# Edge stage of a graph layer rebuilt on one Trainium2 core: node-major sums, one-hot stationary, pieces in place

## The reference, cut to what matters

```python
xn = _layernorm(x)
msg = relu(xn[src] + edge_attr)                 # 106250 x 256
h = xn + zeros.at[dst].add(msg)                 # the node sums
h = relu(batchnorm(h @ W1 + b1)) @ W2 + b2      # 256 -> 512 -> 256, then graph norms
q, k, v = split(xn @ W_qkv + b_qkv)             # q, k centred over channels
k2 = k*k / (sum_c(k*k) + 1e-7); k2 = k2 / norm of k2 over the nodes
q2 = q*q / (sum_c(q*q) + 1e-7); q2 = q2 / norm of q2 over the channels
mix = (v + q2 @ (k2.T @ v) / sqrt(6250)) @ W_out + b_out
x = x + (xn + relu(norms(h))) + mix
x = x + mixture_of_8_experts(_layernorm(x))     # top 2 of 8, hidden 682
```

## Time and profile before

| | |
|---|---|
| median of 3 runs | 2623.18 us (2623.16 to 2633.58) |
| span of the profiled execution | 2627.9 us |
| busy: PE, DVE, ACT, POOL | 1897.2, 1206.7, 818.4, 1251.6 us |
| edge stage, first gather issue of its block to the first issue of the next stage | 92.8 to 1445.2 us |
| `up` of the MLP stage on PE | 1455.1 to 1542.3 us |
| granted clock of the whole span | 0.815 |

### The profile page before, as it was taken

The page is one execution under the profiler, slowest core; times in us unless marked ns, Lnnn a source line. Parts: engine busy times, 40 slices in busy tenths (PEclk is TensorE's granted clock), DMA queues, the critical chain, the costliest instruction groups (busy, mean ns, idle before and its releaser), DMA issues. The chain is left out here.

```text
span 2627.9 us, 43936 instructions
## 1 busy us (share of the span) xinstructions
PE 1897.2 (72%) x12178; PEld 1621.3 (62%) x12179; DVE 1206.7 (46%) x3382; ACT 818.4 (31%) x1643; POOL 1251.6 (48%) x1126
## 2 busy tenths in 40 slices
PE   3566677677665677677775889663429999999993
PEld 3455555446555666566665778552318888888883
DVE  5444444445444554454454344563315445445441
ACT  5122222222221222222222345622314444444441
POOL 1566677667666766666664000225752222222221
PEclk7677788778777887777777899556759999999997
DMA  9555555546455665565554800667932232232234
GB/s 207 181 173 170 169 183 185 166 162 205 160 168 173 197 203 178 176 201 174 185 188 138 252 0 0 179 162 195 261 91 41 44 48 45 44 48 45 44 48 114
DMA packets 234810, 368.27 MB, mean 140 GB/s; under 512 B 96291, under 2 KB 184245, under 8 KB 221332
## 3 DMA queue, kind: packets, MB, share of 16 engines
q1 hardware_dynamic: 147689, 205.63, 25.4%
q0 software_dynamic: 74288, 155.59, 22.2%
q10 hardware_dynamic: 12795, 6.60, 1.3%
HBM read 286.51 MB, written 74.69 MB: 137 GB/s over the span
## 5 line engine op out<-in xcount | busy, mean ns | idle before, releaser
L497 POOL DMA_INDIRECT gathered<-xn_rows,src_index x824 | 908.5, 1103 | 433.6 <-issue 262.7
L729 PE MATMUL bank<-dst_select,message 128*128 128x128 f32 x3328 | 530.9, 318 | 278.4 <-issue 149.2
L729 PEld LDWEIGHTS bank<-dst_select,message 128*128 128x128 f32 x3328 | 494.4, 230 | 359.8 <-issue 291.1
L1637 PE MATMUL bank<-rowsT_parts,expert_weights 128*128 128x256 f16 x3564 | 409.5, 274 | 10.1 <-issue 6.2
L1604 POOL DMA_INDIRECT output_rows<-expert_out,token_index x108 | 167.7, 1553 | 475.3 <-DVE token_index L1757 446.5
L1637 PEld LDWEIGHTS bank<-rowsT_parts,expert_weights 128*128 x3564 | 346.1, 98 | 59.8 <-issue 18.0
L620 ACT ACTIVATE message<-message 128x2048 f32<-128x2048 f32 x104 | 198.7, 1910 | 522.6 <-DVE message L576 327.8
L576 DVE TENSOR_TENSOR message<-gathered,edge_attr 128x2048 f32<-128x2048 f32 x104 | 238.4, 2292 | 201.0 <-DMA gathered<-xn_rows,src_index 171.3
L1650 PE MATMUL bank<-expert_weights,gated_parts 128*128 x1836 | 209.3, 273 | 0.6 <-DVE gated_parts L1752 0.6
L1744 DVE SCALAR_TENSOR_TENSOR gated<-bank,silu 128x512 f32<-128x512 f32 x216 | 120.7, 559 | 163.7 <-ACT silu L1682 162.7
L1650 PEld LDWEIGHTS bank<-expert_weights,gated_parts 128*128 128x128 f16 x1836 | 179.5, 98 | 21.7 <-issue 0.9
(11 more groups left out here) (254 smaller groups left out, 2225.1 us busy)
## 6 DMA issues: line engine op xcount, KB each, us to landing
edge_attr<-in_edge_attr SPq DMA_DIRECT2D x104, 1024.0 KB
dispatched_rows<-empty_row SPq DMA_DIRECT2D x2, 7410.0 KB, 35.7
rows<-dispatched_rows SPq DMA_DIRECT2D x55, 260.0 KB
gathered<-xn_rows,src_index POOLq DMA_INDIRECT x832
xnT_tile<-xnT SPq DMA_DIRECT2D x100, 125.0 KB
raw_weights<-in_L_ffn_w SPq DMA_DIRECT2D x16, 640.0 KB
out<-output_rows SPq DMA_DIRECT2D x1, 6250.0 KB, 21.8
rows_to_send<-token_rows ACTq DMA_DIRECT2D x10, 568.8 KB
```

The costliest lines, as they stand in the source:

```text
L497: pool.indirect_dma_start(out=GA[h][:, e, :], out_offset=None, in_=k.xn_d[:, :], in_offset=bass.IndirectOffsetOnAxis(ap=IDX[h][:, e:e + 1] ...
L729: last = pe.matmul(PE_[h][:, c * WIN:(c + 1) * WIN], MSG[h][:, e, c * 128:(c + 1) * 128], SEL[h][:, e, :], start=e == 0, stop=e == EK - 1)
L1637: last = pe.matmul(bank[:, jj * TT:(jj + 1) * TT], w(e, wp, at + b * step, 128), X16[h][:, xp, b, :], start=n == 0, stop=n == 3 * CB - 1)
```

## The change

- The node sums are held node-major: `node_sum` has 128 nodes on the partitions, 50 tiles of 256 channels. The layernorm writes its rows straight there (7 groups of 7 tiles of 128 rows) and stores them from there; ACT makes only the copy to `xnT`, two tiles at a time.
- The tables come as 104 rows of 1024, are cast on DVE and turned on PE. Gathers take their index from `src_table` itself, and batches 0 and 1 are both issued in the layernorm stage.
- In the edge stage the one-hot is the stationary operand and the message the moving one, 256 columns. The one-hot is made on `dst_partition`, the destination's place in its tile modulo 128, and DVE adds the window to two tiles (`into_tiles`), with a mask in each.
- The add is done in place in `edge_attr`, in 8 instructions of 256 elements; there are three buffers of `edge_attr`.
- The key sums are taken over the normalized rows instead of the values (`rows_in`, loaded again from HBM); the value and output weights are applied once, after the sums (`key_weights`). The second pass makes queries and values node-major, turns the squares on PE, and adds the biases by a matmul with one row.
- All loops of both stages are unrolled. The semaphores of both stages are cleared and freed with one more barrier.
- `up` turns `node_sum` first: 4 transposes and a DVE copy for each of 25 chunks of 256 nodes.

```diff
 def layernorm_stage(k, st):
-    G = 10
-    NG = NT // G
+    G = 7
+    NG = PT // G
...
         def _(pool):
...
-            pool.tensor_copy(k.IDX[0][:, :], k.src[:, 0, :]).then_inc(idx_first, 1)
...
+            pool.wait_ge(src_ready, 2)
+            pool.wait_ge(xn_st, 16 * (NG + 1))
+            for b in range(2):
+                gather(k, pool, b, b)
...
+            for n, work in enumerate((None, table_floats, bases, centred, turned_weights, locals_, products)):
+                norm(n)
+                if work:
+                    work()
...
 def edge_mix_stage(k, st):
         @block.gpsimd
         def _(pool):
-                    pool.wait_ge(idx_ready, b)
-                    pool.wait_ge(added, b + 1)
-                    pool.sem_inc(gathers_begun, 1)
+            for b in range(2, NB):
+                pool.wait_ge(added, b - 1)
+                gather(k, pool, b, b % 2)
         @block.vector
         def _(dve):
+            def add(b):
+                ea, ga = EA[b % 3], GA[b % 2]
+                dve.wait_ge(ea_in[b % 3], 16 * (b // 3 + 1))
+                dve.wait_ge(g_in[b % 2], 16 * EK * (b // 2 + 1))
+                for e in range(EK):
+                    last = dve.tensor_tensor(ea[:, e, :], ga[:, e, :], ea[:, e, :], ALU.add)
+                last.then_inc(added, 1)
...
+                for j, here in enumerate((k.here, k.next)):
+                    u = k.UTn[:, bass.ds(at + j, 1), :].rearrange("p a c -> p (a c)")
+                    last = dve.scalar_tensor_tensor(u, WINP[b % 2][:, 0:C], here[:, b:b + 1], u, ALU.mult, ALU.add)
...
-                    dve.tensor_tensor(MSG[h][:, :, :], GA[h][:, :, :], EA[h][:, :, :], ALU.add).then_inc(added, 1)
-                    dve.tensor_copy(IDX[h][:, :], k.src[:, bass.ds(b + 2, 1), :].rearrange("p a k -> p (a k)")).then_inc(idx_ready, 1)
...
+            for b in range(NB):
+                select(b)
+                if is_tile(b - P2 - 2):
+                    residual(b - P2 - 2)
+                add(b)
+                if b > 0:
+                    into_tiles(b - 1)
+                if is_tile(b - P1):
+                    key(b - P1)
+                if is_tile(b - P1 - 1):
+                    scaled(b - P1 - 1)
         @block.tensor
         def _(pe):
+            def scatter(b):
+                pe.wait_ge(sel_done, b + 1)
+                pe.wait_ge(relu_done, b + 1)
+                if b >= 2:
+                    pe.wait_ge(evac, b - 1)
+                for e in range(EK):
+                    last = pe.matmul(WINP[b % 2][:, 0:C], SEL[b % 2][:, e, :], EA[b % 3][:, e, :], start=e == 0, stop=e == EK - 1)
+                last.then_inc(win_full, 1)
...
-                    for c in range(CB):
-                        for e in range(EK):
-                            last = pe.matmul(PE_[h][:, c * WIN:(c + 1) * WIN], MSG[h][:, e, c * 128:(c + 1) * 128], SEL[h][:, e, :],
-                                             start=e == 0, stop=e == EK - 1)
...
 def gnn_mlp_stage(k, st):
+            def turn(c, h):
...
+                        last = pe.transpose(TP[h][:, b * UP + j * NP:b * UP + (j + 1) * NP],
+                                            k.UTn[:, 2 * c + j, b * 128:(b + 1) * 128], k.ident[:, :])
```

More of the change, by code:

```diff
@@ L387, in edge_mix_stage @@
+            for n, work in enumerate((None, table_turns, base_rows, None, weight_products, None, None)):
+                turn(n)
+                if work:
+                    work()
 def edge_mix_stage(k, st):
     nc, sb, sem, A = k.nc, k.sb, k.sem, k.A
-    two = range(2)
-    EA = [sb(f"edge_attr{h}", [128, EK, C], F32, st) for h in two]
-    GA, IDX, g_in = k.GA, k.IDX, k.g_in
-    MSG = [sb(f"message{h}", [128, EK, C], F32, st) for h in two]
-    SEL = [sb(f"dst_select{h}", [128, EK, WIN], F32, st) for h in two]
@@ L444, in on @@
-    def on(eng):
-        def wrap(f):
-            f.eng = eng
-            schedule(f)
-            return f
-        return wrap
-    def held(eng):
-        eng.wait_ge(ready, READY)
+    two, three = range(2), range(3)
+    EA = [sb(f"edge_attr{h}", [128, EK, C], F32, st) for h in three]
+    GA, g_in = k.GA, k.g_in
+    SEL = [sb(f"dst_select{h}", [128, EK, NP], F32, st) for h in two]
+    XT = [sb(f"rows_in{h}", [128, C], F32, st) for h in two]
+    KB = [sb(f"key{h}", [128, C], F32, st) for h in two]
@@ L529, in kv_scale, with select @@
-            def kv_scale(t, h):
-                dve.wait_ge(ks_done, t + 1)
-                dve.wait_ge(kv_used, t + 1)
-                dve.tensor_scalar(RS[h][:, :], KS[h][:, :], EPS_DIV, None, ALU.add)
+            def select(b):
+                h = b % 2
+                if b >= 2:
+                    dve.wait_ge(win_full, b - 1)
+                for e in range(EK):
+                    last = dve.tensor_scalar(SEL[h][:, e, :], k.iota[:, :], k.dstp[:, b, e:e + 1], None, ALU.is_equal)
+                last.then_inc(sel_done, 1)
@@ new lines, in keys, with key_sums @@
+            def keys(t):
+                v, h = rows_of(t), t % 2
+                if t >= 2:
+                    pe.wait_ge(kb_done, t - 1)
+                for c in range(CB):
+                    last = pe.matmul(KP[h][0:v, 0:C], k.XNT[:, t, c, 0:v], k.wk[:, c, :], start=c == 0, stop=c == CB - 1)
+                last.then_inc(kp_full, 1)
+            def key_sums(t):
+                v, h = rows_of(t), t % 2
+                pe.wait_ge(rs_done, t + 1)
+                pe.wait_ge(k4_done, t + 1)
+                first, done = t == 0, t == PT - 1
+                for q in range(CB):
+                    pe.matmul(MP[q][:, 0:C + 1], K2[t % 3][0:v, q * 128:(q + 1) * 128], VS[h][0:v, :],
+                              start=first, stop=done, skip_group_check=True)
+                pe.matmul(NRM[0:1, 0:C], k.ones[0:v, 0:1], K4[h][0:v, :], start=first, stop=done, skip_group_check=True).then_inc(kv_used, 1)
@@ new lines, in _ @@
+            for b in range(NB):
+                if is_tile(b - P1):
+                    keys(b - P1)
+                if is_tile(b - P1 - 2):
+                    key_sums(b - P1 - 2)
+                if is_tile(b - P2):
+                    query_value(b - P2)
+                if is_tile(b - P2 - 1):
+                    query_turns(b - P2 - 1)
+                if b == FIN:
+                    key_weights()
+                scatter(b)
+                if is_tile(b - P2 - 1):
+                    mixed(b - P2 - 1)
@@ L734, in stray_stage @@
+            for t in range(NB - P2 - 1, PT):
+                query_turns(t)
+                mixed(t)
 def stray_stage(k, st):
```

985 lines of the change are left out of this document (544 added, 441 removed).

## The result

The change took 2668.91 us (median of 4 runs, 2656.88 to 2678.08) against 2628.38 for the kernel before: ratio 1.0156, 95% interval 1.0103 to 1.021. So it is slower, by about 1.6%, where the forecast was 2447. The profiled execution has a span of 2667.6 us against 2627.9.

What follows compares the result with a forecast made beforehand. It took POOL's gather issues in the edge stage, plus holds and gaps, to bound the kernel. 2627.9 + 8.5 (head) - 198 (edge stage) + 12 (tail) + 1 (barrier) = 2451.4, less 4.7 for the median: 2447 us, range 2370 to 2565.

Steps and rivals of the forecast that it cites:

- POOL's own price: Edge stage: POOL's 8 gather issues plus the pieces' hold were to take 10.4 us a batch.
- PE's 27 instructions a batch: Edge stage: PE's instruction count was to fall from 48 to 27 a batch.
- my +12: Tail: the 98 transposes ahead of `up`, with the first turn and copy, were to add 12 us.
- rival F: Transposes don't keep PE's clock up and `up` runs at half speed: 2545 us, chance 0.03.
- the gaps: Edge stage: POOL's idle time from PE's slow stretches, 14 of 4.8 us, +67 us.
- rival C: Edge stage: slow stretches limit columns, not instructions, 10.3 us a gap, 14 times: 2524 us, chance 0.18.
- my own case: Edge stage: a slow stretch limits instructions, 33 in 24 us, costing 4.8 us each; 2405 to 2490 us, chance 0.40.
- Rival E: Edge stage: slow stretches come more often because gathers come denser: 2706 us, chance 0.06.
- B: Edge stage: no gap left, as clock or queue recovers with fewer PE instructions: 2380 us, chance 0.17.
- the head: Layernorm stage up to the third batch's first issue: +8.5 us (-10 to +12), first gather at 82 us.

Runs made afterwards that it cites:

- e13: The change itself, unaltered, timed again on another chip: 2457.97 us, 0.9888 of the kernel before.
- e4: The change with 6 of each batch's 8 sums on PE left out, 15 PE instructions a batch instead of 27: 2591.2 us (before in that set: 2606).
- e1: The change with DVE's residual tile moved behind the add and the window adds: 2672.5 us (before in that set: 2606).
- e3: The change with only an eighth of `edge_attr` loaded from batch 3 on: 2664.9 us (before in that set: 2606).
- e2: The change with the add in one instruction of 2048 elements instead of 8 pieces: 2555.7 us (before in that set: 2606).
- e7: The kernel before with only its add split into 8 instructions of 256 elements: 2806.2 us (before in that set: 2671).
- e18: The change with the residual tile behind the add, as in e1, on a chip without slow stretches: 2453.0 us (before in that set: 2483).
- e9: The one-add version e2 with each table loaded as 96 and 7 rows: 2497.8 us (before in that set: 2483).
- e5: The one-add version e2 with 7 more one-column DVE instructions behind the add: 2604.8 us, first half 575.4 us (before: 2671).
- e8: The one-add version e2 with loads of `x` moved ahead of tables and weights, table work later: first half 576.5 us, total not given.
- e6: The change with a 1024-column fill and a drain on POOL ahead of each batch's gathers: 2807.8 us (before in that set: 2671).
- e10: The change with 5 one-column fills on POOL ahead of each batch's gathers, no drain: 2463.1 us (before in that set: 2483).
- e16: The one-add version e2 timed again beside the change, e13, on one chip: 2535.2 us (before in that set: 2485).

## Why the prediction was wrong, step by step

**Right.** POOL's own price: 10.4 us a batch (10.38 here, 10.4 in e13's first half). PE's 27 instructions a batch ((1242 + 1466) / 102 = 26.5 in the windows above). `up`: first turn at 1481.8, last product done at 1579.1, 97.3 us against 87.2, +10.1 for my +12; rival F is out, since its clock with the turns was 0.99. The Trainium skill (SBUF — State Buffer, Who interferes with whom) infers that `tensor_tensor` doesn't stall descriptor generation; issues of 2.24 us beside one add and 2.96 us beside eight pieces contradict it, as in the earlier trace rows.

**The step that failed: the gaps.** "If a stretch limits instructions, the change gets 33 / 27 = 1.22 batches through" and "at one in 78 us": I took the stretches as given from outside, at a fixed rate, and took each to cost what PE falls behind in it: 14 of 4.8 us. The runs show two things in its place. First, nearly halving PE's instructions did not shorten the gaps: the nine of the first half are 10.4 us on average, in before the seven were 9.3, and in the row 209.00:230.00 PE has 19 instructions in 21 us, or 22 in 24, near the 20 that I had set for rival C and not the 33 of my own case. C's price of 10.3 us a gap came out there; its total (2524) did not. e4 goes further: with 15 instructions a batch the gaps remain, and DVE creeps too, so the limit isn't PE's instructions or columns alone. Second, the stretches answer to the pieces, and so to how POOL issues: on one chip e1 and e3 have 19 long gaps each and e2, with one add, has one; in e7 pieces alone go with 453.9 us of idle time. POOL's idle time for the add was 262.9 us instead of 67. With it the edge stage gave 15 us instead of 198, and these 183 us are most of the 216 between the forecast (-176 on the span) and the measurement (+40). Rival E came nearest, "more often, because gathers come denser", with 0.06 and a price too high (2706 us); e7 bears it out, while the change itself had 19 long gaps against 17. On two other chips none of it is there. That is B's outcome, no slow gaps, but not B's reason: the kernel before, with 48 PE instructions a batch, has none there either.

**The second: a ring that I did not look for,** a round of waits that leads from an operation through other engines to its next instance. I read the new order on DVE (one-hot, residual, add) and said only that the engines stay under 10.4 us. But the residual waits for the mix product, that stands on PE behind the scatter, that waits for relu, that for the add. In the change's second half, the profile on the other chip (e13) shows one turn, from one add to the next:

```profile
1153.85 2.76 DVE L623 TENSOR_TENSOR edge_attr<-gathered,edge_attr 128x256 f32<-128x256 f32 x8
1156.65 1.91 ACT L720 ACTIVATE edge_attr<-edge_attr 128x2048 f32<-128x2048 f32 x1 [0.18 <-DVE edge_attr L623]
1158.66 5.38 PE L795 MATMUL bank<-edge_attr,dst_select 128*128 128x256 f32 x16 [2.61 <-issue]
1164.94 0.48 DVE L695 SCALAR_TENSOR_TENSOR residual_tile<-bank,query_scale,rows_in 128x256 f32<-128x256 f32 x1 [5.44 <-PE bank L860]
1165.84 0.42 DVE L623 TENSOR_TENSOR edge_attr<-gathered,edge_attr 128x256 f32<-128x256 f32 x1
```

From 1153.85 the next add comes at 1165.84: 12.0 us, over POOL's 10.4. No engine is busy for 12 us, which is why sums by engine don't find it. In e13 32 batches of the second half wait for it, 49.1 us in all, and the half takes (603.8 + 1.2) / 54 = 11.2 us a batch (the 1.2 is the last issue). What it costs by itself isn't shown: e18 takes it away, and issues held through all pieces come in its place. The tail is longer too: from the last issue to `up` are 40.1 us (1441.67 to 1481.79) instead of 25.5, +14.6, as the last batches still go round and `up`'s weights are asked for only after them. The ring has only a part in this: without it e18 has 33.8 where e13 has 37.3.

**The third: the head,** +27.2 for +8.5. I put the first gather at 82; it came at 101.2. DVE stood still for the tables, whose loads ran slowly and kept SP's queue busy:

```profile
11.39 20.05 SPq L259 DMA_DIRECT2D src_rows<-in_src  x1
```

```profile
47.90 0.69 DVE L364 CAST dst_rows_f<-dst_rows 104x1024 f32<-104x1024 int32 x1 [29.10 <-DMA src_rows<-in_src]
```

In three stretches (8 to 15, 24.5 to 33 and 36.5 to 41.5 us) only some 24 to 30 GB/s moved. e9's 96 rows removed it: each of SP's issues for a table took 0.2 to 0.7 us, the first gather came at 71.2. I had priced the table loads at nothing since before loads tables too; these have another shape. The Trainium skill (DMA: Bandwidth & Descriptors, Why a DMA increments its semaphore by 16 and not by 1) says that a transfer uses the largest number of engines up to 16 that divides the slowest dimension of both of its sides; by that rule 103 rows give one engine and 96 give 16. The trace agrees: from 36.5 to 41.5 us the DMA share is 0.06, one sixteenth, at 26 GB/s. The rule was there to be read beforehand.

**What stays open.** What the slow stretches are. The loads of `edge_attr` (e3) and the count of DVE's instructions (e5 against e8) are ruled out as causes. What the pieces do to POOL's issuing matters (e2 against e1 and e3). PE's work isn't the cause by itself (e4), though with less of it the stage is shorter; how much of that is the shorter ring isn't shown. Whether it is the slower pace or the hold of POOL beside the one add that helps isn't separated: e6 was too slow, e10 had no effect and ran where there are no slow stretches. Nor is the chip separated from the time: no chip was seen in both conditions, and the sets with slow stretches were the earlier ones.

## What to carry to other kernels

When a stall's cause is unknown, don't carry its rate over to a kernel that loads the same engines differently; bound it by "as often as the faster engine can provoke it" and look whether it exists on another chip, and on the same one later, before tuning against it. After a reorder, walk the waits once round from an operation to its next instance and add the latencies: a ring beats every sum by engine. And look at every engine for the stall, not only at the one whose wait ends it: e4's wait moved from the window add to DVE's own instructions, and that one row's total looked like a cure. Count rows of a transfer, not only bytes: with 103 rows of 4 KB the first gather came at 101.2 us, with 96 and 7 at 71.2.

## What was not expected of the hardware

The same program differs by 7.6% from set to set (before: 2483 to 2671 us). In the two profiles of it all of the difference lies in the stage that gathers: 1324.8 against 1179.7 us, while the tail is 1198.3 and 1198.7. In the sets with slow stretches the window add came up to 24 us after PE's records of its batch, in the case shown 4.9 us after POOL's last issue had ended; and DVE stood up to 10.4 us between two of its own instructions with no wait for another engine (e4). Eight adds of 256 elements instead of one of 2048 cost 135 us on one chip, in the kernel before (e7), and saved 77 on another, in the change (e13 against e16).
